# A third pair of banks and an identity product for the shared heads of layer 1, with the first pass put in another order

## What is computed

```python
B, N, C = x.shape
H, hd = (NUM_HEADS, HEAD_DIM)                  # 16, 16
q = (x @ Wq + bq).reshape(1, B * N, H, hd)
kv = (cond @ Wkv + bkv).reshape(1, -1, 2, H, hd)
...
q = _fq_sym(q, axis=-1)
k = _fq_sym(k, axis=-1)
v = _fq_sym(v, axis=2)
attn = jnp.einsum('bhqd,bhkd->bhqk', q, k)     # 1024 keys for each query
attn = jax.nn.softmax(attn.astype(jnp.float32), axis=-1)
attn = _fq_unsigned(attn, axis=-1)
out = jnp.einsum('bhqk,bhkd->bhqd', attn, v)
```

## Time and profile before

| | |
|---|---|
| median of 3 runs | 1724.72 us (1724.24 to 1726.85) |
| the profiled execution | 1724.53 us |
| its span | 1722.7 us |
| TensorE busy / weight loads | 1429.0 / 924.4 us (83% / 54%) |
| VectorE busy | 1120.9 us (65%) |
| ScalarE busy | 686.2 us (40%) |
| GpSimd busy | 121.4 us (7%) |
| mean granted TensorE clock | 0.879 |

### The profile page before, as it was taken

One profiled execution on the slowest core, in us unless ns is written; L12 is line 12 of the kernel. 1 busy time (PEld: TensorE's weight loads), 2 busy tenths in 40 slices (PEclk: granted clock), 3 DMA queues, 4 the chain that ended last, 5 costly groups with the idle time before them and its releaser, 6 DMA issues.

```text
span 1722.7 us, 25511 instructions
## 1 busy us (share of the span) xinstructions
PE 1429.0 (83%) x9752; PEld 924.4 (54%) x9752; DVE 1120.9 (65%) x2569; ACT 686.2 (40%) x1274; POOL 121.4 (7%) x98
## 2 busy tenths in 40 slices
PE   4899999999999999999989999768985666665665
PEld 1766765765765665675676576447772222222343
DVE  4468467566755755746846756657675777775676
ACT  1353343434434334335335334213444666663111
POOL 2002001001100100200200200030000000000010
PEclk9999999999999999999999999979995555556786
DMA  9100000000000000000000003030002666772000
GB/s 345 49 5 5 16 4 5 10 10 6 10 10 6 10 10 6 10 10 5 1 17 4 5 10 105 19 103 7 7 5 58 132 129 140 134 134 57 7 6 13
DMA packets 160216, 70.11 MB, mean 41 GB/s; under 512 B 137696, under 2 KB 155488, under 8 KB 159584
## 3 DMA queue, kind: packets, MB, share of 16 engines
q1 hardware_dynamic: 158944, 68.13, 15.6%
q10 hardware_dynamic: 1152, 0.36, 0.1%
HBM read 29.67 MB, written 5.24 MB: 20 GB/s over the span
## 4 chain that ended last, share of the span: by engine, by line
PE 65%; DVE 20%; issue 7%; ACT 5%; POOL 1%; DMA 1%; SPq 0%; DVEq 0%; POOLq 0%; ACTq 0%
PE ps_p L1467 13%; PE ps_t L1483 12%; PE ps_t L1489 6%; PE ps_s L1663 6%; DVE w_moe L1390 5%; PE ps_o L1681 4%; PE ps_o L1523 4%; PE ps_s L1505 3%; PE ps_p L1505 3%; PE ps_o L1663 3%; PE ps_o L1637 2%; PE ps_s L1823 2%; PE ps_s L1851 2%; PE ps_o L1823 1%; ACT bigT L737 1%
## 5 line engine op out<-in xcount | busy, mean ns | idle before, releaser
L1483 PE MATMUL ps_t<-ident,probs 128*128 128x128 f32 x1072 | 168.7, 281 | 24.4 <-ACT probs L851 11.7
L737 ACT ACTIVATE probsT<-ps_t 128x512 f32<-128x512 f32 x232 | 137.1, 595 | 129.3 <-PE ps_t L1483 128.9
L1483 PEld LDWEIGHTS ps_t<-ident,probs 128*128 128x128 f32 x1072 | 131.4, 144 | 69.5 <-ACT probs L851 16.9
L765 ACT ACTIVATE probs<-probs 128x512 f32<-128x512 f32 x192 | 120.2, 626 | 104.5 <-DVE probs L994 104.4
L737 ACT ACTIVATE bigT<-ps_t 128x512 f32<-128x512 f32 (+1 forms) x160 | 85.5, 564 | 136.0 <-PE ps_t L1483 132.9
L1467 PE MATMUL ps_p<-w_qkv,xinT 128*128 128x512 f32 (+1 forms) x240 | 107.7, 574 | 31.1 <-DVE row_max L939 18.7
L1663 PE MATMUL ps_s<-w_moe,xbT 128*128 128x352 f32 x352 | 121.7, 470 | 5.3 <-DVE probs L1215 5.3
L1489 PE MATMUL ps_t<-ident_b 128*128 128x512 bf16 x432 | 123.8, 402 | 0.0
L1823 PE MATMUL ps_o<-keys2T,w_moe 48*128 48x512 bf16 x128 | 66.0, 617 | 57.0 <-ACT w_moe L887 56.6
L1390 DVE TENSOR_REDUCE w_moe<-ps_o 128x1 f32<-128x1024 f32 x64 | 78.3, 1223 | 44.4 <-PE ps_o L1823 44.4
L887 ACT ACTIVATE w_moe<-ps_o,w_moe 128x1024 int16<-128x1024 f32 x64 | 77.0, 1203 | 61.8 <-DVE w_moe L1392 60.8
(11 more groups left out here) (301 smaller groups left out, 2705.6 us busy)
## 6 DMA issues: line engine op xcount, KB each, us to landing
w_moe<-in_wT_gu SPq DMA_DIRECT2D x1, 5632.0 KB, 18.9
w_moe<-in_wT_down SPq DMA_DIRECT2D x1, 2816.0 KB, 25.7
w_qkv<-in_wT_qkv SPq DMA_DIRECT2D x1, 2048.0 KB, 9.3
w_out<-in_wT_out SPq DMA_DIRECT2D x1, 2048.0 KB, 19.1
keys<-keys2T SPq DMA_DIRECT2D x8, 256.0 KB, 2.1
keys2T<-keys SPq DMA_DIRECT2D x1, 2048.0 KB, 13.1
w_moe<-w_moe SPq DMA_TRANSPOSE x128, 2.7
w_qkv<-in_wT_qkv SPq DMA_DIRECT2D x2, 512.0 KB, 8.2
```

The source lines that it names most:

```text
L737: nc.scalar.activation(dst, src.bitcast(BF16) if dst.dtype == BF16 else src, ACT.Copy)\
L765: nc.scalar.activation(probs[:, g % 4, :], probs[:, g % 4, :], ACT.Exp, scale=scale)\
L1483: ins = nc.tensor.transpose(dst[:, i * P:(i + 1) * P], src(i), ident_b[:] if bf else ident[:])
```

## The change

It has four parts.

- **Shared heads.** `shared_scores(u)` gives heads the pairs `ps_s`, `ps_o`, `ps_t` in turn, and TensorE waits for the exponentials of head u-3 instead of u-2. Ahead of each head's scores stands `dense(psum[:, 1, :], 1)`: one product of 512 bf16 columns of copies of the identity, into a bank that the scores then overwrite.
- **Rounding.** All nine pieces move to steps 2 to 10 of the first pass, one a step, between the bias of the values and `queries`.
- **Seam.** The wait for `scales1` moves to the last pass. The memsets move: the stacks' to expert 12 of tile 7, the values' into steps 0 and 1; that of lane 1's `qk_pad` goes (it now lies in `v_all`). VectorE quantises the values in step 1, not GpSimd.
- **First pass.** `x3` and `q1` stand ahead of `o1` and `out1`; `qk0` ahead of the second pair of `p`; one bias comes earlier on VectorE.

```diff
@@ transposes1 / projections1
-        keys += [("o1", q), ("x3", p), ("qs", r)]
-        keys += [("p", None if s is None else G1 * s + g) for g in (0, 1)] + [("x4", q)]
-        keys += [("p", None if s is None else G1 * s + g) for g in (2, 3)] + [("qk0", p), ("qk1", p)]
+        keys += [("x3", p), ("o1", q), ("qs", r)]
+        keys += [("p", None if s is None else G1 * s + g) for g in (0, 1)] + [("x4", q), ("qk0", p)]
+        keys += [("p", None if s is None else G1 * s + g) for g in (2, 3)] + [("qk1", p)]
...
-        keys += [("out1", q), ("q1", p), ("k1", p), ("v1", p), ("q2", q)]
+        keys += [("q1", p), ("out1", q), ("k1", p), ("v1", p), ("q2", q)]
...
-PIECES = KD * I1 // PIECE
-LAST_DVE = {0: ("gate", 0), 1: ("gate", 1), 2: ("gate", 2), 3: ("up", 0), 4: ("up", 1), 6: ("up", 2)}
+PIECES = [(name, j) for name in ("gate", "up", "down") for j in range(KD * I1 // PIECE)]
+ROUND_FROM = 2
...
+        def shared_scores(u):
+
+            return (ps_s, ps_o, ps_t)[u % 3]
@@ VectorE, experts of layer 0
-                    if not project and e in LAST_DVE and debug > 3:
-                        round_fp8(*LAST_DVE[e])
+                    if not project and e == E - 4 and debug > 3:
+                        for lane in lanes:
+                            step(nc.vector.memset(lane.stack, 0.0))
@@ VectorE, layer 1
-            for lane in lanes:
-                link1(nc.vector.memset(lane.v_wide, 1.0))
-            for ap in (lanes[1].qk_pad, lanes[0].stack, lanes[1].stack):
-                link1(nc.vector.memset(ap, 0.0))
             dve.wait_ge(ld_w["l1"], 16 * 9)
-            dve.wait_ge(ld_w["scales1"], 16 * 2)
...
                 if p is not None:
+                    if p < LANES:
+
+                        link1(nc.vector.memset(lane_of(p).v_wide, 1.0))
                     add_bias(p, 2)
-                if i < PIECES:
-                    round_fp8("down", i)
+                if i == 1:
+                    dve.wait_ge(ld_values, 16)
...
+                if ROUND_FROM <= i < ROUND_FROM + len(PIECES):
+                    round_fp8(*PIECES[i - ROUND_FROM])
@@ TensorE, shared heads
-                    psum = ps_s if u % 2 == 0 else ps_o
+                    psum = shared_scores(u)
...
-                    if u >= 2:
-                        pe.wait_ge(exp2, u - 1)
+                    if u == 2:
+
+                        turned("qs", LAST)
+                    if u >= 3:
+                        pe.wait_ge(exp2, u - 2)
+
+                    dense(psum[:, 1, :], 1)
                     for n in range(2):
```

More of the change, by code:

```diff
@@ L874, in _ @@
                     exps(s, 1)
+                if p is not None:
+                    turned("qk0", p, lane_of(p).qkT[:, 0:4, :])
+                if s is not None:
                     probs_turned(s, 1)
                 if p is not None:
-                    for j in range(2):
-                        turned(f"qk{j}", p, lane_of(p).qkT[:, 4 * j:4 * j + 4, :])
+                    turned("qk1", p, lane_of(p).qkT[:, 4:8, :])
             for u in range(TILES * H1):
@@ L1356, in _ @@
                     shift_pair(s, 0)
+                if p is not None:
+                    add_bias(p, 0)
                 if q is not None:
@@ L1769, in _ @@
                          bf=True)
+                if p is not None:
+                    turned("x3", p)
+                    project(L1, 0, ("q1", p), lane_of(p).xinT, w_qkv1, 0, D)
                 if q is not None:
```

51 lines of the change are left out of this document (23 added, 28 removed).

## The result

| | before | after |
|---|---|---|
| median | 1724.86 us | 1667.57 us (1666.06 to 1668.13, 4 runs) |
| ratio to before, 95% interval | | 0.9665 (0.9648 to 0.9681) |
| span of the profiled execution | 1722.7 us | 1665.7 us |
| mean granted TensorE clock | 0.879 | 0.892 |

The change takes off 57 us. 1647.5 was forecast; the measured time lies in the range, 20 us above the forecast, on the value that I had put to the rival "swinging clock" (1667). That agreement is chance. The clock did not swing: it stayed low all through the shared heads. What happened is rival 1's mechanism at a lower price than I gave it, and with more won ahead of the heads.

What follows compares the result with a forecast made beforehand. Different bounds by stage; in the shared heads, latency around two pairs of banks. 1724.5 - 51.5 (heads) - 10 (tile 7) - 15.5 (seam) + 1.5 (rounding) = 1649.0, less 1 to 2 for half-clock steps: 1647.5 us; range 1632 to 1682.

Steps and rivals of the forecast that it cites:

- swinging clock: Shared heads: TensorE's clock swings between both levels, stage about 219 us, total 1667 (1657 to 1680); chance 0.20.
- rival 1: Shared heads: clock stays at 1.2 GHz, TensorE bound at 1.81 to 1.90 us a head, total 1680 to 1692; chance 0.13.
- Third pair of banks: Shared heads: latency 1.31 us a head, VectorE sets the pace at 1.39; stage 200 instead of 251.5 us, gain 51.5.
- late landings: Shared heads: some ten transposing transfers land late and delay sums by 1.3 us each, 13 us in all (0 to 25).
- Identity product: Shared heads: adds 0.43 to 0.52 us a head on TensorE at 1.2 GHz; hidden at 2.4 GHz, so costing nothing.
- I take the high clock: Shared heads: full occupation raises TensorE's clock to 2.4 GHz, and about 65% occupation then holds it; forecast's chance 0.58.
- rival 3: Shared heads: transposing transfers become the bound at 2.34 us an issue, stage 299.5 us, total 1745; chance 0.03.
- milder form: Shared heads: transposing transfers stretch to only 1.6 us, which lies in the upper half of the forecast's range.
- Tile 7's experts: Rounding out of tile 7: TensorE needs 16.5 to 19.3 us for what took 27.5; gain 8 to 11, taken as 10.
- Seam: Normalised tile to first reduction: 5 to 6.5 us remain of 23.05; net gain 15.5, between 12 and 17.
- Rounding in the steps: First pass, steps 2 to 10: 3.0 us pieces fill 2.83 us idle ahead of `queries`; 1.5 us charged in all.
- Order of the first pass: First pass: reordering saves some 0.4 us and loses some 0.5; taken as 0, between -5 and +5 for eight steps.

Runs made afterwards that it cites:

- six buffers: Six instead of five buffers for the turned exponentials, against the changed kernel without identity product, with five buffers and the first pass in its old order: 1627.30 us.
- the burst: 24 identity products once, ahead of the first shared head, added to the changed kernel, which keeps its one product a head: 1671.47 us, ratio 0.9687.

## Why the prediction came out as it did

**Third pair of banks: right, in mechanism and size.** "1.39 is above 1.31, so VectorE sets the pace" and a stage of 200 us are what the kernel without the product shows: 200.1 us and reductions 1.38 us apart; 50.3 us gained against 51.5. That is at the low clock, though, and in a kernel that leaves out the product. The late landings were put at 13 us, the weakest number of the sum: VectorE idled 14.5 us ahead of twelve reductions there, and 1.576 a head less the 1.447 with six buffers is 0.129, times 128 heads 16.5 us.

**Identity product: the step that failed.** It is the sentence "I take the high clock". Of the two arguments for it, the first fell at once: full occupation at the low level did not raise the clock, since TensorE was busy 20.00 of 20 us at 0.50 (1300 to 1320 us). The second, that a clock once high would hold at 65% occupation, got no support: behind the burst it was lost at the fourth head, with TensorE busy 2.74 of 4 us, although 2.56 of 4 had kept it in layer 0. Since no sum had been made yet, the steady round was never seen at the high clock. In place of the high clock stood 0.50 through the stage, and the product cost 21.6 us in it. The argument against, thin scores and sums, was in the text, and I gave the low clock a chance of 0.13. Why the clock stayed low is open. What these runs show is that TensorE's busy time in the profile does not decide it alone: 20.00 of 20 us did not raise it, with one product or, after the fall, with three. What raised it was the burst and the opening of the kernel with three products, before any sum. Whether rows of the scores, columns of the sums, or both count, was not separated; nor was the mix from the idle time behind which the clock fell both times.

**Rival 1's price: too high.** I added 0.43 to 0.52 us to 1.38 and got 1.81 to 1.90 a head. The cycle is 1.72, with 0.59, 1.03 and 0.38 in it, which overlap at their ends; with the heads where something is late 1.746. That is 28.6 us gained, not 8 to 20. Together with 29.3 us ahead of the heads, instead of the 25.5 in my sum (my text on rival 3 says 27, which leaves out the 1.5 for the rounding), this puts the low clock at 1667 instead of 1680 to 1692, which is why the total looks like rival 2's.

**Rival 2, the swinging clock: it did not happen.** Every stretch of the stage shows 0.50. By the Trainium skill, "TensorE: Matmul & The Clock Gate", section "A second HAM failure mode: psum-queue depth-cycling", a kernel of 512-column products that cycles through banks, with frequent short pauses, swings between both levels. No kernel here does so in this stage: after has hardly a pause and stays at 0.50, the one without the product has pauses (TensorE busy 135 of 160 us) and stays at 0.50 too, and the three-product kernel shows one fall and no return. In the last pass of after the clock does go to and fro: 1.00 from 1580 to 1584 us, 0.50 from 1588 to 1592, 1.00 from 1596 to 1600.

**Did a high clock even matter?** No. My text made it the condition for the 51.5 us, since the product had to be hidden. Without the product VectorE is the bound at 1.2 GHz too. The first 48 heads took 1.584 us each at 1.00 with three products and 1.582 at 0.50 with none. Only the product itself, put in to raise the clock, made the clock matter.

**Rival 3, transfers: not in that form.** With six buffers an issue on SP took 1.26 us in the median at 1.45 us a head. The milder form, sums that wait for a late landing, is real, and two more buffers take nearly all of it away.

**Tile 7's experts: right, the size was 2.8 us short.** I took TensorE to need 16.5 us at least, from 19.28 us with 2 to 3 of half clock in it; it needs 14.5. The gain is 12.8 (13.0 by the run that undoes it), beyond my 8 to 11.

**Seam: right, 2.7 us short.** 4.9 us remain between normalised tile and first reduction, at the lower end of my 5 to 6.5. The 2 us that I charged for quantising on VectorE are 0.4. Put back into the changed kernel, the wait for the scales costs 14.0 us with the clock that it loses. Before, VectorE idled only 7.35 us in it, since the memsets ran first, so the 14.0 can't be taken off the 18.2 to price the rest: the memsets and the rounding piece with its 5.15 us operation were not undone one by one.

**Rounding in the steps: right in place, at least 1.2 us short.** The piece fills the idle time ahead of `queries` (2.83 to 0.54 us), and six of the nine cost 2.7 us by the run that takes them back, where I had charged 1.5 for all. The last one, between the last `queries` and the first shared reduction, delays that reduction by 0.4 at its own place: the scores were ready at 1284.73, the reduction starts at 1285.19. Most of the rest lies in the same end of the pass.

**Order of the first pass: 0 was taken, it is a loss of 2.6.** That is within the -5 to +5, and a step grew by 0.32 us, below the 1 us that I had named as the sign of a mistake. Rounding and order together lose 5.3 us by these runs, and the pass grew by 1.7: the other 3.6 were won elsewhere in it. Part is the start, 1.3 us shorter up to the first attention output that TensorE turns; the rest was not found.

**The whole.** 22.9 us less than forecast in the heads, 1.7 in the first pass and 0.9 ahead of tile 7's experts stand against 5.5 us more in the experts and the seam: 20 us. So the total in the range is in part luck: the mechanism of the heads was wrong by 22.9 us, and gains that I had put too low made up for about a quarter of that.

## What to carry to other kernels

Before paying for a higher TensorE clock, ask which engine is the bound once the real latency is gone: here the third pair of banks moved the bound to VectorE, and a filler product only moved it back to TensorE. A TensorE that is busy all the time is no sign that the clock will rise; try the mix itself, and leave the filler out if it does not. When a loop through a transfer has irregular landings, try one or two buffers more behind the landing: here the first was worth 11 us and the second 2.5, with a transfer share that still rose from 0.85 to 0.94.

## What the runs showed of the hardware

- TensorE, busy 216 of 220 us (1286 to 1506 us of after, in parts 20.00 of 20), stayed at a granted clock of 0.50, with one product of 128 rows by 512 columns, two of 48 rows by 512 and eight of 16 columns a head. With three full products a head the clock rose to 1.00 in the opening of the stage, held for some 85 us, and then stayed at 0.50 for 190 us of unbroken work. The Trainium skill, "TensorE: Matmul & The Clock Gate", section "Part 1: The HAM clock gate", has the clock follow how busy TensorE has been; by the busy time of these profiles that does not hold here. This busy time counts products of 48 rows or of 16 columns like full ones.
- Both falls to 0.50 inside the stage came behind a pause of TensorE: 1.26 us after the burst (2.74 of 4 us busy), and 1.36 us for a late transfer with three products (2.64 of 4). Whether the pause or the mix decides was not tried.
- A wait of 11.2 us on TensorE cost another 3 us through the clock behind it.
- A 7.14 us operation of GpSimd left VectorE's reductions and subtractions from PSUM at 0.69 us and its memset at 0.38, while in the kernel before a rounding operation from SBUF to SBUF stood for 5.15 us beside it and ended 0.3 us after it. The next rounding operation, 0.43 us elsewhere, took 1.99 us beside GpSimd's last one of 1.94 us and ended 0.3 us after it too. Which property makes one stand and not the other was not tried.
- Transposing transfers of 256 KB were issued every 1.45 us (six buffers) with a median issue of 1.26 us and moved 181 GB/s at a share of 0.94, and some landings still took 5 us:

```profile
L654 SPq DMA_TRANSPOSE w_out<-w_moe x128: 1231/1259/2676, 1286.9 to 1470.9; - x128
...
DMA to landing us min/median/max: 2.7/2.8/5.3
```
